# Two-layer graph kernel: VectorE unpacks adjacency tiles at two earlier places in each step

## The reference

```python
h = relu(layernorm(x))
x1 = swish((adj @ h) @ W0 + b0)
x = x + swish((adj @ x1) @ W0 + b0)
h = relu(layernorm(x))
d = sum(adj + I, axis=1) ** -0.5
x = x + (((adj + I) * d[:, None] * d[None, :]) @ h) @ W1.T + b1
```

## Time and profile before

| what | value |
|---|---|
| median of 3 runs (lowest to highest) | 1496.16 us (1495.65 to 1497.3) |
| the profiled execution: its own time, its span | 1496.04 us, 1494.2 us |
| first sweep | to about 800 us of the span |
| second sweep | about 800 to 1028 us |
| third sweep | about 1028 us to the end |
| PE busy over the span | 1397.5 us (94%) |
| DVE busy over the span | 965.4 us (65%) |

### The profile page before, as it was taken

The page is one execution under the profiler, slowest core; times in us unless marked ns, Lnnn a source line. Parts: engine busy times, 40 slices in busy tenths (PEclk is TensorE's granted clock), DMA queues, the critical chain, the costliest instruction groups (busy, mean ns, idle before and its releaser), DMA issues.

```text
span 1494.2 us, 18073 instructions
## 1 busy us (share of the span) xinstructions
PE 1397.5 (94%) x6598; PEld 652.0 (44%) x6598; DVE 965.4 (65%) x2271; ACT 628.2 (42%) x751; POOL 40.7 (3%) x30
## 2 busy tenths in 40 slices
PE   1677999999999999999999998888999999999998
PEld 0233444444444444444444444444444444444444
DVE  5889999999888886786774677566523333233331
ACT  4888887788777676666560122121000000000000
POOL 0100000000000000000000111110000000000000
PEclk9789999999999999999999999999999999999999
DMA  8789999999999898787760111110000000000000
GB/s 293 272 337 399 407 405 407 396 405 412 397 382 370 332 355 352 296 356 281 299 252 29 36 57 57 50 64 29 29 22 22 15 22 22 14 15 29 15 15 23
DMA packets 77165, 297.72 MB, mean 199 GB/s; under 512 B 5648, under 2 KB 38928, under 8 KB 44304
## 3 DMA queue, kind: packets, MB, share of 16 engines
q1 hardware_dynamic: 58304, 284.71, 49.1%
q10 hardware_dynamic: 18768, 11.80, 2.4%
HBM read 284.69 MB, written 11.80 MB: 198 GB/s over the span
## 4 chain that ended last, share of the span: by engine, by line
PE 75%; DVE 12%; DMA 8%; ACT 3%; issue 2%; SPq 0%; POOL 0%; DVEq 0%; ACTq 0%
PE acc_ps L540 19%; PE acc_ps L541 19%; PE acc_ps L481 9%; PE acc_ps L482 9%; DMA ring<-adj 8%; PE early_ps L454 5%; PE early_ps L453 5%; PE z_ps L436 3%; DVE marks L778 2%; PE kept_ps L462 2%; PE kept_ps L463 2%; ACT unused L649 2%; DVE ring L305 1%; DVE count_a L813 1%; ACT node_b L610 1%
## 5 line engine op out<-in xcount | busy, mean ns | idle before, releaser
L649 ACT ACTIVATE unused<-ring 128x2048 uint8<-128x2048 uint32 x256 | 488.6, 1909 | 119.4 <-DMA ring<-adj 108.2
L481 PE MATMUL acc_ps<-marks,node_a 128*128 128x512 fp8e4 x1024 | 396.0, 387 | 68.8 <-DVE node_a L771 48.3
L482 PE MATMUL acc_ps<-marks,node_a 128*128 128x512 fp8e4 x1024 | 395.8, 386 | 1.8 <-issue 1.8
L540 PE MATMUL acc_ps<-ring,node_a 128*128 128x512 fp8e4 x1024 | 388.1, 379 | 2.1 <-DVE ring L305 1.9
L541 PE MATMUL acc_ps<-ring,node_a 128*128 128x512 fp8e4 x1024 | 388.1, 379 | 0.0
L778 DVE TENSOR_SCALAR marks<-ring 128x2048 uint8<-128x2048 f32 x256 | 314.7, 1229 | 73.9 <-DMA ring<-adj 46.2
L305 DVE TENSOR_SCALAR ring<-bits 128x256 uint32<-128x256 uint32 (+1 forms) x784 | 158.3, 280 | 153.8 <-PE acc_ps L541 153.6
L481 PEld LDWEIGHTS acc_ps<-marks,node_a 128*128 128x128 f16 x1024 | 101.6, 99 | 207.6 <-issue 95.4
L690 ACT ACTIVATE nT<-acc_ps 128x512 f32<-128x512 f32 x16 | 9.6, 597 | 425.6 <-PE acc_ps L541 425.6
L540 PE MATMUL acc_ps<-ring,node_b 128*128 128x512 fp8e4 x416 | 160.1, 385 | 16.7 <-DVE ring L305 16.7
L541 PE MATMUL acc_ps<-ring,node_b 128*128 128x512 fp8e5 x416 | 160.1, 385 | 0.0
(11 more groups left out here) (111 smaller groups left out, 993.6 us busy)
## 6 DMA issues: line engine op xcount, KB each, us to landing
ring<-adj SPq DMA_DIRECT2D x256, 1024.0 KB, 7.5
xch<-x SPq DMA_DIRECT2D x16, 256.0 KB, 2.9
xn_scratch<-xnew ACTq DMA_DIRECT2D x16, 256.0 KB, 2.3
xch<-xn_scratch SPq DMA_DIRECT2D x16, 256.0 KB, 2.8
out<-xnew ACTq DMA_DIRECT2D x16, 256.0 KB, 2.3
part_scratch<-stage ACTq DMA_DIRECT2D x13, 256.0 KB, 5.4
marks<-part_scratch SPq DMA_DIRECT2D x13, 256.0 KB, 3.1
b_sb<-b SPq DMA_DIRECT2D x2, 64.0 KB, 7.2
```

Of the source, the lines that this page charges most:

```text
L481: nc.tensor.matmul(acc_ps[c % 2][:, :], hi_of(node_a16, j), byte, start=(j == 0), stop=False)
L482: last = nc.tensor.matmul(acc_ps[c % 2][:, :], lo_of(node_a16, j), byte, start=False, stop=(j == NB - 1))
L540: nc.tensor.matmul(into[:, :], hi_of(node, j), byte.bitcast(E4), start=opens, stop=False)
L649: nc.scalar.activation(unused[:, :], slot(g).bitcast(U32), ACT.Sign, accum_out=nz_count[:, g:g + 1]).then_inc(counted, 1)
```

## The change

A helper counts how many pieces of a step PE has done by a given block. The unpacking loop becomes a function, `unpack_upto(end)`, and is called at two more places: at the start of a turn, ahead of `finish_second` or `finish_third`, up to `FIRST_PIECE[k] + RING`; and within `finish_second(k)`, between the bias and the wait for the sigmoid, up to the pieces that step k+1 has done by its `PROJECT_BLOCK`, plus `RING`. The set of instructions is the same; their order on DVE differs.

```diff
+def pieces_done(k, block):
+
+    done, blocks = FIRST_PIECE[k], 0
+    for m in range(FIRST_PIECE[k], FIRST_PIECE[k + 1]):
+        blocks += len(list(PIECES[m].blocks()))
+        if blocks <= block:
+            done += 1
+    return done
...
+            def unpack_upto(end):
+                for m in range(made[0], min(end, len(PIECES))):
+                    if m == FIRST_PIECE[NC]:
+                        dve.wait_ge(ident8_set, 1)
+                    unpack(m)
+                    made[0] = m + 1
+
             def finish_second(k):
                 n, par, t = SECOND_ORDER[k], k % 2, NC + k
                 xn = half(xnew, par)
                 add_bias(t)
+                unpack_upto(pieces_done(k + 1, PROJECT_BLOCK[k + 1]) + RING)
                 dve.wait_ge(sig_ready, t + 1)
...
-            made = RING
+            made = [RING]
             for k in range(2 * NC):
+                unpack_upto(FIRST_PIECE[k] + RING)
...
-                while made < min(len(PIECES), FIRST_PIECE[k + 1] + RING - 1):
-                    if made == FIRST_PIECE[NC]:
-                        dve.wait_ge(ident8_set, 1)
-                    unpack(made)
-                    made += 1
+                unpack_upto(FIRST_PIECE[k + 1] + RING - 1)
```

## The result

| | median (lowest to highest) | runs | ratio to before, 95% interval |
|---|---|---|---|
| before | 1496.32 us (1495.65 to 1497.3) | 4 | |
| changed | 1469.04 us (1468.63 to 1470.41) | 4 | 0.9819 (0.9802 to 0.9836) |
| changed, measured again | 1469.37 us (1467.79 to 1470.12) | 5 | 0.9815 (0.9802 to 0.9828), beside a before of 1496.26 |

The change makes the kernel 27 us faster. The direction and the mechanism were as forecast. The forecast was 25.0 us, and the result lies 0.4 us under the low end of the range, 1469.4. So the range was wrong, and the question behind it is where 2 us more came from than the sum had.

The account below looks back on a forecast made before the run. PE sets the end and DVE holds it up in the second sweep: 26.6 us lost there, less 1.3 and 0.3 left, gives 25.0 off 1496.04, so 1471.0, stated as 1471.1 us. Range 1469.4 to 1475.0.

Parts of the forecast that it names:

- The waits for a piece: Second sweep: nine PE waits for a piece that DVE unpacks behind z, all to go, worth 20.0 us.
- T: Moment when PE is free again after a project; first piece behind z is there at T + 7.63 plus its unpacking.
- The clock: Second sweep: half clock after waits of 5.19 and 3.47 us, for twelve and eight matmuls; 4.1 us to get back.
- The floor: Step 1 to the project in step 17: at most 26.6 us to give back, so at best 1469.4 us.
- the first sweep is not touched: Before 825 us: the order on DVE differs only from turn 1 on, so nothing changes there.
- What is left: Before the projects in steps 7, 9 and 11: `nT` late by 1.3 us, plus 0.1 for each late project.
- part two: Even steps: one unpacking moved between bias and gate, gaining 0.7 us per even step where `nT` was late.
- Block 60: Step 16, PE reads step 15's node values: POOL ends by T + 13.6, needed at T + 14.24; loss taken as 0.
- Rival 1: Part two gives nothing or takes a little (`nT` late, or wait at block 60): 1473.5, up to 1475 us; chance 0.12.
- Rivals 2 and 3: 2: loads take the waits' place, 1476 to 1490 us, chance 0.03; 3: waits move to another cause, 1496, 0.02.
- Rival 4: Eight even steps: gate stands behind a piece whose slot isn't free, 6.9 us each before slack; 1521 us, chance 0.02.

Follow-up runs that it names:

- skip_8_13: Changed kernel with both added `unpack_upto` calls left out in turns 8 and 13: 1479.09 us, ratio 0.9888 to before.
- early_only: Changed kernel without the call between bias and gate, the one ahead of the wait for z kept: 1472.13 us, ratio 0.9836 to before.
- mid_only: Changed kernel without the call ahead of the wait for z, the one between bias and gate kept: 1475.03 us, ratio 0.9856 to before.
- hold_16: Changed kernel with two more pieces unpacked between bias and gate in turn 16, the second waiting for a slot: 1479.14 us, ratio 0.988 to before.

## Why the prediction was right and where it was wrong

**The waits for a piece: right.** The formula from DVE's rows (T + 7.63 + the unpacking, less the blocks that PE still has) gave 20.0 us; with the fourth slot filled ahead they are gone to the last one, and where the calls are left out again in one turn the computed wait comes back (5.19, 3.20 and 3.46 us of idle).

**The clock: the term that was mis-sized.** The step that failed is "twelve matmuls up to 965.25 and eight up to 1009.52 [...] 4.1 us". It is true of that one execution. In four of five profiles of the same kernel there is a third fall, after the wait of 3.21 us in step 8, worth 1.5 to 1.7 us; the term is 5.4 to 5.8 us there. The row that showed a wait of 3.21 us with no fall behind it, next to one of 3.47 with a fall, should have been a bound and not a zero: the two are nearly one length. With 1.7 us more, the sum is 26.7. The fall came back when the wait in step 8 was put back alone with that in step 14 (skip_8_13), so its price does hang on these waits; why it stayed out in one execution is open.

**The floor as low end of the range: wrong for the same reason, and for a second.** "No order on DVE can give back more" than 26.6 us was worked out from one execution and then used against a median of others. The part ahead of the change, while `adj` is loaded, moves by 3.3 us from execution to execution; "the first sweep is not touched" was right and gave no reason to let it weigh nothing. This profile of the changed kernel had it 1.1 us shorter. The spread of the runs shown (1495.65 to 1497.3) was there to widen the range by. That the execution predicted from lay within 0.3 us of the median all the same was luck. It had some 1.5 us less of low clock than the others, and started step 1 at 825.0, where the medians leave about 823.8 (an estimate: 1496.3 less 1.8 around the span, 432.0 behind the project in step 17, and a stretch of 238.7).

**What is left: the right places, a little too much.** `nT` is late at the projects in steps 7, 9 and 11 and nowhere else, but costs 1.1 us in all (11.62, 11.36 and 11.62 us against 11.25, and 0.1 behind each) where 1.6 were forecast. The waits without part two were sized right: in early_only these three intervals are 12.42, 12.15 and 12.41 us, so 1.2, 0.9 and 1.2 over 11.25, as computed. What was too small is the worth of part two, 0.8 us each in place of 0.7: DVE starts the unpacking 0.61 us after a bias that takes 0.69 (894.67 to 895.28 above), and so gains 0.08 beside the 0.69 of waiting. The rest is rounding in the list. With the 1.5 to 1.7 us of the clock and these 0.5, the forecast of 25.0 becomes 27.0 to 27.2, against 27.0 from the stretches.

**Part two: right in its worth, not in where it acts.** 2.8 us against 2.5. The prediction had a piece between bias and gate in the eight even steps alone; in the trace turns 13 and 15 have one too, so ten in all, and DVE's waits for the sigmoid go from 16 to 6. No load, no slot and no bias held anything up that PE noticed. DVE waits 3.7 us for the load in `prepare_out(0)`, where about 3 were forecast. Every bias starts at T + 0.20 as before, in turns 11 and 15 without any idle time of DVE left; in early_only these two come later, at T + 0.46 and T + 0.85, where 0.3 us was to be the most that a bias is late.

**Block 60: right, and as tight as said.** POOL's last low part, DVE's unpacking beside it, and PE at block 60 of step 16 in the changed kernel:

```profile
1028.20 1.83 POOL L418 TENSOR_TENSOR node_a<-y,node_a 128x512 f16<-128x512 f32 x1 [12.14 <-ACT node_a L691]
```

```profile
1025.71 3.32 DVE L317 TENSOR_SCALAR ring<-bits 128x256 uint32<-128x256 uint32 x16
```

```profile
1030.93 0.38 PE L552 MATMUL acc_ps<-ring,node_a 128*128 128x512 fp8e4 x1
```

With T = 1016.68 POOL ends at 1030.03, T + 13.35 (forecast: 13.6 if held up, 12.9 if not), and 0.9 us are to spare where 2.9 were. It ends 1.0 us after DVE's run of sixteen instructions (1025.71 + 3.32 = 1029.03), not after the instruction that it met. The page of the Trainium skill ("SBUF — State Buffer", section "SBUF: two separate sides") is borne out in that GpSimd is shut out, and the length goes by the row: it waited for the run. The two experiments that put one or two pieces more in that place (mid_only, hold_16) lost 1.1 and 6.1 us of idle time there; most of the latter is the wait for a slot.

**The rivals.** Rival 1 in its first form is early_only, 2.8 us from the changed kernel; in its second (a wait at block 60) it is 0.9 us away. Rivals 2 and 3 left no trace. Rival 4 is real as a mechanism (hold_16), and excluded here by the count.

## What to carry to other kernels

Where one engine runs an order written by hand, list for each buffer slot when it is free and when its filling stands in the queue: a filling that stands behind a long dependent chain costs the consumer that chain, and it can be moved ahead at no cost if its slot is free by then. A wait of the matrix engine is dearer than its length once it nears those after which the clock was seen to fall, and such a row from one execution is a sample: price a wait of 3.2 us beside one of 3.5 us with the fall as well as without. A saving worked out from one profile gets the spread of the runs on both ends, even where the sum looks like a bound.

## What the runs showed of the hardware that was not expected

- The granted clock (1.2 in place of 2.4 GHz, starts 0.43 us apart) fell after a PE wait of 3.2 us in four of five profiles of one kernel and in the one of skip_8_13, and not in the fifth; after 3.5 us and more it fell every time, thirteen of thirteen. It starts with the first matmul behind the wait or up to 1.3 us later, and lasted 7 to 12 matmuls, 1.5 to 2.4 us of loss. The Trainium skill ("TensorE: Matmul & The Clock Gate", section "What's actually happening") says of the rise of the clock that its point varies from run to run of one kernel. These rows show such a variation in the falls too, and in the stretch behind them: eleven or twelve matmuls after the same wait in step 10. What decides it in one execution was not tried.
- After any of the waits that are left (0.2 us), after those of 1.0 to 1.8 us in early_only and mid_only, and after those of 1.2 and 1.9 us in the five profiles of the kernel before, the clock stayed.
- The first 300 us of the kernel, in which PE still waits for marks made of `adj`, varied by 3.3 us over 14 profiles, and everything behind them up to step 1 of the second sweep repeated to 0.01 us, though the loading of `adj` goes on there.
